# The read of K's first half ahead of the fetch of Q's next weights, and a buffer of its own for K's reads

## What is computed

```python
qkv = jax.nn.silu(hidden_states @ qkv_w.T)          # 512 -> 3 * 32 * 128
def step(kv, blk):
    cq, ck, cv = blk
    scores = jnp.einsum('bhnd,bhmd->bhnm', cq, ck) * diag_decay
    intra = jnp.einsum('bhnm,bhmd->bhnd', scores, cv)
    inter = jnp.einsum('bhnd,bhde->bhne', cq * q_decay, kv)
    kv_next = kv * block_decay + jnp.einsum('bhnd,bhne->bhde', ck * k_decay, cv)
    return (kv_next, intra + inter)
...
gate = jax.nn.sigmoid(hidden_states @ gate_w.T)
return gate * rms_normed_attention @ out_w.T
```

## Time and profile before

| | before |
|---|---|
| median of 3 runs | 2727.16 us (2718.6 to 2730.34) |
| the profiled execution's own time | 2721.68 us |
| its span, first to last instruction | 2719.5 us |
| PE busy | 2443.0 us (90%) |
| POOL / DVE / ACT busy | 1635.7 / 1383.9 / 1126.0 us |
| TensorE's granted clock, mean | 0.951 of 2.4 GHz |
| DMA | 103 GB/s over the span |

### The profile page before, as it was taken

The page is one execution under the profiler, slowest core; times in us unless marked ns, Lnnn a source line. Parts: engine busy times, 40 slices in busy tenths (PEclk is TensorE's granted clock), DMA queues, the critical chain, the costliest instruction groups (busy, mean ns, idle before and its releaser), DMA issues.

```text
span 2719.5 us, 38204 instructions
## 1 busy us (share of the span) xinstructions
PE 2443.0 (90%) x12256; PEld 2061.5 (76%) x12256; DVE 1383.9 (51%) x2454; ACT 1126.0 (41%) x1666; POOL 1635.7 (60%) x1311
## 2 busy tenths in 40 slices
PE   4799999999999999999999999999999998689996
PEld 3677777777777777777877777777777777568884
DVE  5545555555555555545444544444445445544447
ACT  6533344444344443334443444444444343543333
POOL 4666666666666666656666666666666664534344
PEclk8899999999999999999999999999999999899998
DMA  3533333333333333353333332333333334100101
GB/s 116 194 109 116 116 116 110 107 105 111 115 115 106 111 114 102 116 203 130 105 105 104 104 104 95 101 102 99 96 101 104 104 104 148 67 24 29 41 23 62
DMA packets 145541, 281.09 MB, mean 103 GB/s; under 512 B 20560, under 2 KB 86096, under 8 KB 143184
## 3 DMA queue, kind: packets, MB, share of 16 engines
q1 hardware_dynamic: 139440, 269.39, 30.6%
q10 hardware_dynamic: 6048, 11.01, 1.2%
HBM read 199.60 MB, written 80.74 MB: 103 GB/s over the span
## 4 chain that ended last, share of the span: by engine, by line
PE 49%; DMA 12%; issue 11%; POOL 10%; ACT 6%; DVE 6%; SPq 3%; ACTq 0%; POOLq 0%; DVEq 0%
PE proj L1752 32%; PE yp L1752 8%; DMA kv_tok<-k_blocks 8%; PE sc L1795 4%; DMA k_blocks<-pd 4%; POOL w_lo L554 3%; SPq L370 3%; POOL w_lo L547 2%; PE sc L1808 2%; PE sc L1818 2%; POOL h_lo L686 2%; PE sc L1821 2%; ACT kd L901 1%; DVE pd L1340 1%; ACT sq L908 1%
## 5 line engine op out<-in xcount | busy, mean ns | idle before, releaser
L1752 PE MATMUL proj<-xb,w_hi 128*128 128x512 f32 x3584 | 1199.7, 417 | 183.1 <-DVE vf L1306 149.6
L1752 PEld LDWEIGHTS proj<-xb,w_hi 128*128 128x128 f32 x3584 | 681.3, 199 | 328.5 <-DVE vf L1306 162.3
L1752 PE MATMUL proj<-xb,w_lo 128*128 128x512 f32 x1792 | 726.6, 405 | 0.0
L554 POOL TENSOR_TENSOR w_lo<-ws,w_hi 128x1024 fp32r<-128x1024 f32 x128 | 307.1, 2400 | 258.2 <-ACT w_hi L854 258.2
L1752 PEld LDWEIGHTS proj<-xb,w_lo 128*128 128x128 f32 x1792 | 353.3, 197 | 81.0
L1387 DVE TENSOR_TENSOR g<-sc,g 128x512 f32<-128x512 f32 x128 | 88.5, 692 | 482.7 <-ACT sq L908 482.7
L569 POOL TENSOR_TENSOR qd<-q,table 128x512 f32<-128x512 f32 x128 | 162.9, 1284 | 203.3 <-ACT q L894 203.3
L901 ACT ACTIVATE kd<-kv_tok,table 128x512 f32<-128x512 f32 x128 | 85.4, 714 | 418.4 <-DMA kv_tok<-k_blocks 418.4
L547 POOL TENSOR_TENSOR w_lo<-raw,w_hi 128x768 fp32r<-128x768 f32 x128 | 235.7, 1842 | 4.5 <-ACT w_hi L848 1.6
L560 POOL TENSOR_TENSOR ow_lo<-kv_tok,ow_hi 128x1024 fp32r<-128x1024 f32 x32 | 76.4, 2388 | 251.3 <-ACT ow_hi L862 251.3
L1394 DVE TENSOR_TENSOR y<-yp,y 128x512 f32<-128x512 f32 x240 | 164.7, 686 | 96.1 <-PE yp L1752 94.1
(11 more groups left out here) (161 smaller groups left out, 4220.7 us busy)
## 6 DMA issues: line engine op xcount, KB each, us to landing
raw<-w_attn SPq DMA_DIRECT2D x128, 512.0 KB, 3.6
k_blocks<-pd SPq DMA_DIRECT2D x64, 512.0 KB, 3.5
kv_tok<-k_blocks SPq DMA_DIRECT2D x256, 128.0 KB, 3.3
v_blocks<-vf SPq DMA_DIRECT2D x64, 512.0 KB, 2.6
kv_tok<-v_blocks SPq DMA_DIRECT2D x256, 128.0 KB, 2.8
kv_tok<-w_out SPq DMA_DIRECT2D x32, 512.0 KB, 4.3
check<-w_ints ACTq DMA_DIRECT2D x42, 256.0 KB, 3.4
table<-tables SPq DMA_DIRECT2D x32, 258.0 KB, 3.2
```

The source lines that it names most:

```text
L554: pool.tensor_tensor(w_lo[:, slot, S_1:S_4 + 1], ws[:, :, :, :], w_hi[:, slot, S_1:S_4 + 1].bitcast(F32), ALU.subtract).then_inc(wlo_s_don ...
L1752: last = pe.matmul(psum, s, m, start=start and n == 0, stop=n == len(terms) - 1, skip_group_check=more)
```

## The change

Three things: K's reads get a buffer of their own (`k_tok`), and `kv_tok`, renamed `v_tok`, keeps V's reads and the output weights; the waits of the reads follow from that; and in `window` on SP `k_read(w, 0)` is called ahead of `weights(w + 1, QQ, ...)`. The new buffer takes 1024 of the 1536 float32 elements per partition of what had been spare room.

```diff
-        sb("spare", [P, 3, SEG], scope=two)
-        kv_tok = sb("kv_tok", [P, QUADS, 2, CH, QUAD], scope=two)
+        k_tok = sb("k_tok", [P, QUADS, 2, CH, QUAD], scope=two)
+        sb("spare", [P, SEG], scope=two)
+        v_tok = sb("v_tok", [P, QUADS, 2, CH, QUAD], scope=two)
...
             def k_read(n, s):
                 sp.wait_ge(k_out, 16 * (2 * n + 2 - s))
-                if s == 1:
-                    wait(sp, owlo_done, n)
-                else:
-                    sp.wait_ge(kd_done, 4 * n + 2)
+                wait(sp, kd_done, 4 * n + 2 - 2 * s)
                 for b in range(QUADS):
-                    sp.dma_start(kv_tok[quad(b)].rearrange("t i h c d -> t i (h c d)"),
+                    sp.dma_start(k_tok[quad(b)].rearrange("t i h c d -> t i (h c d)"),
...
             def v_read(n, s):
                 sp.wait_ge(v_out[s], 16 * (n + 1))
                 if s == 0:
-                    sp.wait_ge(kd_done, 4 * n + 4)
+                    wait(sp, owlo_done, n)
                 else:
                     sp.wait_ge(v_done, 4 * n + 2)
...
                 k_write(w, 0)
+                k_read(w, 0)
                 if next_weights:
                     weights(w + 1, QQ, pair + 1 if not isinstance(pair, int) else (pair + 1) % PAIRS)
-                k_read(w, 0)
                 v_write(w, 1)
```

More of the change, by code:

```diff
@@ L242, in sandwich_kernel @@
                                                                 b=QUADS, h=2, c=CH)
-        ow = kv_tok[:, :, :, :, :].rearrange("p i h c d -> p (i h c d)").rearrange("p (h n) -> p h n", h=2)
+        ow = v_tok[:, :, :, :, :].rearrange("p i h c d -> p (i h c d)").rearrange("p (h n) -> p h n", h=2)
         one = ExitStack()
@@ L385, in v_read @@
                 for b in range(QUADS):
-                    sp.dma_start(kv_tok[quad(b)].rearrange("d i h c t -> d i (h c t)"),
+                    sp.dma_start(v_tok[quad(b)].rearrange("d i h c t -> d i (h c t)"),
                                  v_blocks[s, :, :, b].rearrange("i d n -> d i n")).then_inc(v_in, 16)
@@ L900, in k_decay @@
                 wait(act, contrib_done, att_until(n - 1, s, h))
-                act.activation(kd[:, s, h].rearrange("p c (i d) -> p i c d", i=QUADS), kv_tok[:, :, h],
+                act.activation(kd[:, s, h].rearrange("p c (i d) -> p i c d", i=QUADS), k_tok[:, :, h],
                                ACT.Copy,
@@ L1348, in turn_v @@
                 dve.transpose(v[:, s, :, h].rearrange("p c (i d) -> p c i d", i=QUADS),
-                              kv_tok[:, :, h].rearrange("p i c t -> p c i t")).then_inc(v_done, 1)
+                              v_tok[:, :, h].rearrange("p i c t -> p c i t")).then_inc(v_done, 1)
             def decay_scores(n, s, h):
```

## The result

| | before | changed |
|---|---|---|
| median, us | 2725.0 (4 runs, 2718.6 to 2730.3) | 2530.1 (4 runs, 2528.1 to 2534.3) |
| ratio to before | | 0.9288, 95% interval 0.9263 to 0.9312 |
| span of the profiled execution | 2719.5 | 2529.1 |
| granted clock, mean of the span | 0.951 | 0.976 |

The change takes 195 us away, 7.1%. The forecast was 2530 us.

A forecast was written before the change was run, and what follows sets the result against it. PE's wait for V's s3, held by order on SP and ACT, bounds the kernel; 7.8 us a window less new stalls of 0.5 and 0.8 gives 6.5, times 30 windows 195 us off: 2530 us, range 2485 to 2600.

The forecast's parts named there:

- The stall and its cause: V's product 3 on PE waits 4.99 us per window for DVE's s3, behind ACT's K decay, held by SP's order.
- The period without a wait: Window 31 lacks the fetch between; from it, one window with no PE wait takes 62.6 us instead of 70.41.
- The clock: PE's slow clock behind the stall, some 2 us a window, comes back; stalls of a microsecond run at full clock.
- The new stalls: Two formerly covered chains make PE wait in each window: 0.5 us for G's s1, 0.8 for K's s3.
- G's s1: G's product 2 on PE waits for ACT's s1, itself behind POOL's low parts of g: 0.5 us a window.
- K's s3: K's product 3 on PE waits for DVE's s3, at the end of V's way round: 0.8 us, bounds 0 to 2.
- the landing of V's reads: In V's way round, each of the two reads was taken to land 5.1 us after its issue.
- The sum: Per window 7.8 - 0.5 - 0.8 = 6.5 us off, period 63.9; times 30 windows, 195 us; 2530 us.
- the clock that stays low: Two short PE waits a window still bring the clock to 0.50, keeping 2 us each window: 2587 us; chance 0.08.
- the waits that move: V's reads land later and ACT and DVE come later, so new stalls are 1.5 and 2 us: 2593 us; chance 0.17.
- Absorption: Both newly exposed chains fit without any stall, as in window 31; period 62.6 us, 2488 us in all; chance 0.06.
- The slower case: The read, held at the head of SP's queue, holds the fetch and V's writes behind it: 2827 us; chance 0.03.

The follow-up runs named there:

- the first held kernel: Changed kernel with K's second read held until POOL has made the low parts of G's first four blocks, still ahead of the fetch: 2566.3 us, ratio 0.9441.
- POOL's order: POOL makes g's low parts ahead of Q's last two decays: 2509.2 us on the changed kernel, 2722.9 on the kernel before, 2509.7 with read moved and single buffer.
- the one edit made there: Changed kernel with g's low parts ahead of Q's last two decays, plus the second batch's first two activation loads ahead of V's writes: 2510.1 us, ratio 0.9239.

## Why the prediction was right

**The stall and its cause**: right. The order alone gives all, the buffer nothing, and with the decay moved on ACT the read may stay where it was. So reading K early is sufficient for the gain, and not necessary.

**The period without a wait**, 62.6 us from window 31: measured 62.7 in the kernels in which PE has no gap. One window that the loop's edge had left without the obstacle gave the number.

**The clock**: right. Some 2 us a window came back with the stall. The Trainium skill (TensorE: Matmul & The Clock Gate, "A second HAM failure mode: psum-queue depth-cycling") tells of a kernel in which frequent short idle times between groups of matmuls made the clock swing. Taken over to this kernel it would have kept the two microseconds. No such swing shows here: in the changed kernel, with waits below 1 us in the loop, and in the first held kernel, with 1.4 on the mean, the stretches show 1.00. What one short idle time had suggested held for a whole loop.

**The new stalls**: the places were right and the sizes were not. G's s1, taken as 0.5 us a window, showed 0.25 to 0.5 in half of the windows; K's s3, taken as 0.8, showed 0.2 to 0.3 in five. The mis-sized term is the landing of V's reads. I took 5.1 us for each, from the second read of one window. SP's and DVE's rows of a window of the second batch, changed kernel:

```profile
1526.10 1.74 SPq L384 DMA_DIRECT2D v_tok<-v_blocks  x4
...
1532.29 1.73 SPq L384 DMA_DIRECT2D v_tok<-v_blocks  x4
```

```profile
1530.31 0.71 DVE L1346 STREAM_TRANSPOSE v<-v_tok 128x512 f32<-128x512 f32 x1 [1.41 <-DMA v_tok<-v_blocks]
...
1536.84 1.31 DVE L1346 STREAM_TRANSPOSE v<-v_tok 128x512 f32<-128x512 f32 x2 [2.83 <-DMA v_tok<-v_blocks]
```

They land in 4.2 and 4.6 us, 1.4 less in sum than taken, which is more than the 0.8 of stall. Over windows 1 to 30 the medians are 4.2 and 4.75. Where the second read landed late, the stall was there: in window 14 the two took 4.24 and 5.95 us (1003.21 to 1007.45, 1009.43 to 1015.38), in sum what I had taken, and PE waited 0.26 us for K's s3. That is still less than 0.8, so the landing is most of the error and not all of it.

**The sum** came out as the median to a tenth of a percent, and partly by luck. The 30 periods gave 196 us, for 195 forecast. But 24 ordinary ones (windows 2 to 14, 18 to 30) gave 6.7 each, where 6.5 was forecast, and the two around the second batch's loads only 4.4 each, which the prediction took as ordinary. The error of the stalls and that omission cancel. The profiled spans differ by 190.4 us only: six of the 196 are given back at the two ends, and that is no more than the scatter there. In the twelve profiles, of kernels old and new, window 1's decay starts between 146.4 and 150.7 us, and the stretch from window 31's to the end takes 460 to 467 us; of the three with the old order and the full stall one has 460.1 and two 464.8 and 464.9.

**The rivals**: the clock that stays low and the waits that move did not come. The second is real as a mechanism, since POOL's order is worth 20 us more once the stall is gone; its stalls were a tenth of what the rival set. Absorption is what the kernels with POOL's order show in the loop, at 2509 us where the rival said 2488. The slower case had no part in it: the read went 0.08 us after the decay that it waits for, and the fetch behind it was held no longer than before.

Open: what POOL's order gives at the second batch's loads and by which queue, since the profiles scatter there by several microseconds and the one edit made there changed nothing.

## What to carry to other kernels

When an engine waits for data that has nothing to do with the transfer at the root of the chain, look at what is queued behind the waiting instruction: moving the transfer up or moving its consumer down are then the same edit, and here each gave the whole 7.1%. Search the program's edges, first and last turns of the loop, for a turn that runs without the obstacle; its row gives the new period before anything is built. And an edit to a chain that a longer stall covers (POOL's order: nothing before, 20 us after) has to be tried again once the stall is gone.

## What the runs showed of the hardware

A stall's price rose faster than its length. Waits of 1.4 us a window cost about themselves, with the clock at 1.00 over the stretch; of 3.1 us, 114 us for 92 of stalls more, with 1.2 GHz behind 21 of 31; of 5 us, 2 us of slow clock behind each.

K's reads of 128 KB, half of them issued right behind a 512 KB fetch, landed in 3.3 us by the median; in the changed kernel, where none is, the page has

```profile
k_tok<-k_blocks SPq DMA_DIRECT2D x256, 128.0 KB, 2.8
```

The kernel that holds them until POOL is done, ahead of the fetch, has 2.8 as well, so it is the fetch in front and not the point in the window at which they go. The Trainium skill (DMA: Bandwidth & Descriptors, "Issuing engines are not separate DMA queues") says that DMAs run on the same 16 engines and interleave, whichever engine issues them; the slower landing fits that, though no run here shows the interleaving itself. So a fetch that nobody needs for 20 us, ahead of a read that is waited for, cost two things here: 9 us in SP's queue and about 1 us in the landing of the four reads.
